# Folding a MoE output projection into the expert weights on chip, during the convolution

## What is computed

```
def _L3_ffn_ref(X, We, be, Wr, br, Wo, bo):
    ...
    router_weights = jax.nn.softmax(router_logits, axis=-1)
    top_k_weights, top_k_indices = jax.lax.top_k(router_weights, TOP_K)
    expert_outputs = jnp.einsum('bsd,ehd->bseh', X, We) + be
    ...
    combined = jnp.sum(top_k_weights[..., None] * gathered, axis=2)
    out = jnp.einsum('bsd,hd->bsh', combined, Wo) + bo
    return out
...
    t = t + _L3_ffn_ref(_ln_t(t), L3_ffn_We, L3_ffn_be, L3_ffn_Wr, L3_ffn_br, L3_ffn_Wo, L3_ffn_bo)
```

## Time and profile before

| | us |
|---|---|
| time, median of 3 runs | 751.39 (750.92 to 751.60) |
| the profiled execution: its own time | 752.36 |
| the profiled execution: span of its instructions | 750.6 |
| PE busy in the span | 637.6 (85%) |
| DVE busy | 471.3 (63%) |
| ACT busy | 320.1 (43%) |
| POOL busy | 143.5 (19%) |

### The profile page before, as it was taken

How to read it: one execution, slowest core, us unless ns; L and a number is a source line. 1 busy time by engine, 2 the same in 40 slices (tenths; PEclk the granted TensorE clock), 3 DMA queues, 4 the chain that set the end, 5 groups by cost and what they waited for, 6 DMA issues and landing times.

```text
span 750.6 us, 11202 instructions
## 1 busy us (share of the span) xinstructions
PE 637.6 (85%) x4168; PEld 396.0 (53%) x4230; DVE 471.3 (63%) x1259; ACT 320.1 (43%) x545; POOL 143.5 (19%) x126
## 2 busy tenths in 40 slices
PE   6543666349699999999999989999999999999987
PEld 3411225236366666666666655565655656564543
DVE  4777555685776776676677675737567473746433
ACT  3254554015355556555555553433434244343110
POOL 2230001572533133212203212020201100000000
PEclk9766777678799999999999999999999999999999
DMA  9300001986774995796597588246090730000000
GB/s 354 134 0 0 0 0 17 124 106 91 68 104 74 85 115 82 65 126 88 65 107 101 83 71 106 22 86 56 22 120 1 110 32 15 1 14 1 15 5 24
DMA packets 83230, 50.53 MB, mean 67 GB/s; under 512 B 4036, under 2 KB 82628, under 8 KB 82884
## 3 DMA queue, kind: packets, MB, share of 16 engines
q1 hardware_dynamic: 83176, 49.81, 46.8%
HBM read 35.11 MB, written 14.68 MB: 66 GB/s over the span
## 4 chain that ended last, share of the span: by engine, by line
PE 62%; DVE 10%; ACT 4%; issue 3%; DMA 2%; SPq 1%; POOL 0%; DVEq 0%; ACTq 0%
PE ps L1145 13%; PE ps L1031 10%; PE ps L1022 7%; PE ps L1091 4%; PE ps L1102 4%; PE ps L1087 3%; PE ps L1070 3%; PE ps L1062 3%; PE ps L1116 3%; DVE acc L1376 2%; PE ps L1014 2%; DVE nparts L1311 2%; PE ps L1156 2%; PE ps L1109 2%; PE ps L1065 2%
## 5 line engine op out<-in xcount | busy, mean ns | idle before, releaser
L1302 DVE TENSOR_REDUCE nmax<-ps 128x2 f32<-128x512 f32 (+1 forms) x192 | 130.7, 688 | 103.5 <-PE ps L1070 62.4
L1198 ACT ACTIVATE PT<-ps 128x512 f32<-128x512 f32 x192 | 114.9, 600 | 120.9 <-PE ps L1091 118.9
L1145 PE MATMUL ps<-wm,xnT 128*128 128x512 f32 x256 | 124.6, 616 | 0.6
L958 POOL TENSOR_TENSOR rstd<-ve,fix 128x2 f32<-128x2 f32 x32 | 22.2, 695 | 356.2 <-DVE ve L1264 356.2
L1192 ACT ACTIVATE QS<-ps 8x1024 bf16<-8x1024 f32 x64 | 65.1, 1017 | 40.2 <-PE ps L1075 39.4
L1376 DVE SCALAR_TENSOR_TENSOR acc<-ps,gate,acc 128x256 f32<-128x256 f32 x128 | 61.6, 481 | 29.6 <-PE ps L1145 27.3
L1091 PE MATMUL ps<-QS,KS 110*128 110x256 bf16 (+3 forms) x512 | 74.7, 248 | 0.0
L994 POOL TENSOR_TENSOR parts<-rest,fix 128x512 bf16<-128x512 f32 x30 | 38.1, 1269 | 159.9 <-DVE rest L1282 105.7
L1145 PEld LDWEIGHTS ps<-wm,xnT 128*128 128x128 f32 x256 | 45.9, 193 | 41.3 <-issue 39.0
L1022 PE MATMUL ps<-xnT,wt 128*128 128x256 f32 x256 | 65.5, 403 | 1.4 <-ACT xnT L1171 1.4
L1087 PE MATMUL ps<-fixb 128*128 128x256 bf16 (+1 forms) x192 | 60.6, 316 | 0.5 <-ACT QS L1192 0.3
(11 more groups left out here) (195 smaller groups left out, 967.9 us busy)
## 6 DMA issues: line engine op xcount, KB each, us to landing
parts_dram<-parts SPq DMA_DIRECT2D x32, 384.0 KB, 3.2
QS<-parts_dram SPq DMA_DIRECT2D x96, 128.0 KB
KS<-parts_dram SPq DMA_DIRECT2D x96, 128.0 KB, 9.8
wt<-wt_dram SPq DMA_DIRECT2D x1, 2562.0 KB, 13.1
wm<-wm_dram SPq DMA_DIRECT2D x1, 2449.0 KB, 18.4
xc<-x_dram SPq DMA_DIRECT2D x8, 256.0 KB, 5.0
out_dram<-res SPq DMA_DIRECT2D x8, 256.0 KB, 2.1
w<-w_dram SPq DMA_DIRECT2D x1, 845.0 KB, 7.4
```

The costliest lines, as they stand in the source:

```text
L1145: mm = pe.matmul(d, normT(stage, batch)[:, c, t * P:(t + 1) * P], M("We", c * EXPERTS * CH + e * 2 * CH, 2 * CH), start=(c == 0), stop=(c ...
L1198: act.activation(PT[:, n % PT_RING, :], bank(piece), ACT.Exp).then_inc(drain(piece), 1)
L1302: dve.tensor_reduce(group[:, 0, :] if part == 0 else group[:, 1, 2 * part - 2:2 * part], bank(piece).rearrange("p (j n) -> p j n", n=w_), ...
```

## The change

Wo is multiplied into the eight experts' weights and into the biases once, during the convolution block. Per expert PE transposes its four 128x128 blocks (turn_expert), ACT copies them to SBUF, PE multiplies them with Wo in four products of 128x256 (fold_expert), and ACT copies the result back over the expert's place in wm. PSUM banks for this are picked from those that the convolution leaves free at the time (TURN_BANK, FOLD_BANK); SBUF comes from tensors whose contents are no longer needed (xp, ph, pool_w). The load of wm is issued ahead of that of wt.

In the transformer block the piece FO is gone with its products, its ACT copy and its bank. CT now writes the result itself: ACT drains it with the two bias steps. The residual, which FO's identity products added, is added when acc is opened: GB is drained by DVE (acc = PSUM + xt) and no longer by ACT. The expert products themselves are as before, over changed contents of wm.

```diff
-        ("E", 3, 5, 39), ("E", 3, 6, 40), ("E", 3, 7, 41), ("CT", 3, 0, 43), ("FO", 3, 0, 45)),
+        ("E", 3, 5, 39), ("E", 3, 6, 40), ("E", 3, 7, 41), ("CT", 3, 0, 43)),
...
+            turned_we = (xp[:, 0, :], xp[:, 1, :], ph[:, :])
+            turned_be = pool_w[:, 0, 0:NC2 * EXPERTS]
+            TURN_BANK = (2, 3, 4, 6, 7, 0, 6, 3)
+            FOLD_BANK = (5, 2, 0, 1, 2, 4, 5, 6)
...
+                sp.dma_start(wm[:], wm_in).then_inc(wm_loaded, 16)
                 sp.dma_start(wt[:], wt_in).then_inc(wt_loaded, 16)
-                sp.dma_start(wm[:], wm_in).then_inc(wm_loaded, 16)
...
+                def turn_expert(e):
+                    for hh in range(NC2):
+                        for c in range(NC2):
+                            mm = pe.transpose(ps[:, TURN_BANK[e], hh * CH + c * P:hh * CH + (c + 1) * P],
+                                              expert(e)[:, c, hh * P:(hh + 1) * P], F("ident"))
+                    mm.then_inc(fold_turned, 1)
+                def fold_expert(e):
+                    pe.wait_ge(fold_turned_out, e + 1)
+                    for c in range(NC2):
+                        for hh in range(NC2):
+                            mm = pe.matmul(ps[:, FOLD_BANK[e], c * CH:(c + 1) * CH],
+                                           turned_we[e % 3][:, hh * CH + c * P:hh * CH + (c + 1) * P],
+                                           M("Wo", hh * CH, CH), start=(hh == 0), stop=(hh == 1))
+                    mm.then_inc(fold_done, 1)
...
+                pe.wait_ge(wm_loaded, 16)
+                for e in range(3):
+                    turn_expert(e)
+                pe.wait_ge(g_out, 1)
+                for e in range(2):
+                    fold_expert(e)
                 pe.wait_ge(weights_ready, 1)
...
+                fold_expert(2)
                 pe.wait_ge(tern_summed, 1)
...
+                for e in range(3, 6):
+                    pe.wait_ge(z_out, e - 2)
+                    turn_expert(e)
+                pe.wait_ge(z_out, 4)
+                fold_expert(3)
+                pe.wait_ge(z_out, 5)
+                fold_expert(4)
                 pe.wait_ge(z_out, 8)
+                turn_expert(6)
+                turn_expert(7)
+                fold_expert(5)
+                fold_expert(6)
                 all_max(0, 1)
+                fold_expert(7)
...
-                if kind == "GB":
-                    full(act, piece)
-                    full(act, ("CT", stage, batch - 1, 0))
-                    copy_out(flat(acc))
...
+                if kind == "GB":
+                    full(dve, piece)
+                    full(dve, ("CT", stage, batch - 1, 0))
+                    dve.tensor_tensor(flat(acc), bank(piece), flat(xt[:, par]), ALU.add).then_inc(drain(piece), 1)
...
                 if kind == "CT":
-                    full(act, piece)
-                    full(act, ("FO", stage, batch - 1, 0))
-                    copy_out(flat(accT))
-                if kind == "FO":
                     full(act, piece)
                     wait(act, "out_stored", before(piece, 2))
```

More of the change, by code:

```diff
@@ L472, in _ @@
                     for q in range(4):
+                        if o == 0 and q == 2:
+                            pe.wait_ge(folded, 3)
                         if o == 0 and q == 3:
@@ L496, in _ @@
                     mm.then_inc(conv_done, 1)
+                pe.wait_ge(fold_turned_out, 9)
+                for c in range(NC2):
+                    mm = pe.matmul(ps[0:EXPERTS, BE_FOLD_BANK, 0:CH], turned_be[:, c * EXPERTS:(c + 1) * EXPERTS],
+                                   M("Wo", c * CH, CH), start=(c == 0), stop=(c == 1))
+                mm.then_inc(fold_done, 1)
                 all_max(1, 2)
+                pe.wait_ge(folded, 9)
                 for k, (src, wgt) in enumerate(((hp1, dwq), (hp2, w2q))):
@@ L527, in _, with expert_turned, expert_folded @@
             def _(act):
+                def expert_turned(e):
+                    act.wait_ge(fold_turned, e + 1)
+                    act.activation(turned_we[e % 3], ps[:, TURN_BANK[e], :], ACT.Copy).then_inc(fold_turned_out, 1)
+                def expert_folded(e):
+                    act.wait_ge(fold_done, e + 1)
+                    act.activation(expert(e), ps[:, FOLD_BANK[e], :].rearrange("p (c n) -> p c n", c=NC2),
+                                   ACT.Copy).then_inc(folded, 1)
                 act.wait_ge(w0_loaded, 16)
@@ L854, in build @@
             acc = lb("acc", [P, 2, CH])
-            accT = lb("accT", [P, NC2, PIX])
             res = lb("res", [P, 2, NC2, PIX])
@@ L946, in sync_piece @@
                             .then_inc(sems[f"stack_loaded{n}"], 16)
-                if kind == "FO":
+                if kind == "CT":
                     wait(sp, "out_stored", before(piece))
@@ L1150, in tensor_piece @@
                     mm = turn4(acc)
-                if kind == "FO":
-                    drained(pe, ("CT", stage, batch, 0))
-                    for o in range(NC2):
-                        for c in range(NC2):
-                            pe.matmul(d[:, o * PIX:(o + 1) * PIX], M("Wo", c * CH + o * P, P), accT[:, c, :],
-                                      start=(c == 0), stop=False)
-                        for t in range(2):
-                            mm = pe.matmul(d[:, o * PIX + t * P:o * PIX + (t + 1) * P], xt[:, par, t, o * P:(o + 1) * P],
-                                           F("ident"), start=False, stop=(t == 1))
                 if kind in JOBS:
@@ L1325, in vector_piece @@
                     if kind == "PR" and stage == 2:
-                        full(dve, ("FO", 3, batch - 2, 0))
+                        drained(dve, ("GB", 3, batch - 2, 0))
                     old = flat(X[:, 2 * batch:2 * batch + 2, :])
```

47 lines of the change are left out of this document (41 added, 6 removed).

## The result

| | before | after |
|---|---|---|
| median of the runs timed side by side, us | 751.22 (750.92 to 751.60) | 729.20 (728.43 to 729.73) |
| the profiled execution: own time / span | 752.36 / 750.6 | 728.74 / 727.0 |
| from the span's start to batch 0's GB products | 448.10 | 448.19 |
| from there to the end | 302.5 | 278.8 |

A forecast was written before the change was run, and what follows sets the result against it. TensorE was taken to bound the second half, while the convolution waits on DVE and ACT. Terms -21.8 + 0 + 0 + 0.1 - 1.7 + 0.9 = -22.5 us gave 729.0 us, range 725.0 to 735.0.

The forecast's parts named there:

- Part 1: Transformer block: dropping FO saves 2.61 us in each of seven batches and 3.57 us at the end, -21.8 us.
- Rival B: Second half: PE's gain is half given back because DVE or the ring of six PSUM banks ends the waits; 739.8 us, chance 0.07.
- 42.0 us in the second half: Sign of being right: batch periods of 42.0 us in the second half, with PE still above 95% busy.
- Part 2: Transformer block: moving GB's drain from ACT to DVE costs 0 us, bounds -0.8 to +5.6 over 8 batches.
- Part 3: Convolution, before L451: folding experts 0 and 1 fits PE's idle 6.53 us, 0 us, bounds 0 and +2.3.
- Part 4: Convolution, PE's 1.62 us before L468: folding expert 2 at the full clock costs +0.1 us, bounds 0 and +1.8.
- Part 5: Convolution, z products: with the idle gap filled, four records no longer run at half clock, -1.7 us, bounds -1.7 and 0.
- Part 6: Convolution, around L481: folding experts 3 to 7, starting at the low clock, costs +0.9 us, bounds 0 and +6.5.
- A: Convolution: the clock does not follow, the first fold runs half at 1.2 GHz, z gains nothing; 733.7 us, chance 0.13.
- C: Convolution: the folding is not hidden at all, 35.5 us at half clock; 765 us, chance 0.02.
- D: Convolution: the clock stays up through folding experts 3 to 6, and first tap products start at full speed; 726.0 us, chance 0.12.
- E: Transformer block: FO was hidden anyway, so only the last batch's 3.6 us would go; 747.8 us, chance 0.02.

The follow-up runs named there:

- e4_slot: The changed kernel with one PSUM bank of the ring of six skipped where FO stood, nothing computed differently: 732.37 us, 0.9743 of before.
- experiment 4: Changed kernel with needless TensorE products before the last gate transposes (726.03 us), then with expert 2 early and expert 6 late too (725.14), then four more products (724.82).
- e3_gb_dve: The kernel before with only GB's drain moved from ACT to DVE, which adds the residual: 751.79 us, 1.0003 of before.
- e7_filler: The changed kernel with three needless 128x512 products on PE ahead of the last batch's gate transposes: 726.03 us, 0.9665 of before.
- e1_no_fold: Convolution block of before (no folding, Wo left out) with the transformer block of after: 727.59 us, 0.968 of before.
- e1_again: The kernel of e1_no_fold, without any folding, run once more beside the last experiments: 727.27 us, 0.9678 of before.
- after_again: The changed kernel itself, nothing altered, run once more beside later experiments: 729.82 us, 0.9705 of before.
- e2_fold_only: Convolution block of after, with all of the folding, and the transformer block of before, FO included: 751.47 us, 1.0005 of before.
- e10_all_warm: e9_all plus four more needless 128x512 products behind the transposes of experts 3 to 5: 724.82 us, 0.9642 of before.
- e9_all: Changed kernel with expert 2 folded before sc's transposes, expert 6 behind the first all_max, three needless products before the last gate transposes: 725.14 us, 0.9649 of before.

## Why the prediction was right, part by part

The profiled execution lost 752.36 - 728.74 = 23.6 us, where the sum said 22.5. By stretches it is 23.7 in the transformer block (21.8 predicted) and +0.1 in the convolution (-0.7 predicted). The total came out well partly because errors of the terms stood against each other.

- **Part 1, FO (-21.8): right.** The periods of e4_slot show 2.61 to 2.63 us a batch, and the end lost 3.58 where 3.57 was predicted. What the step left out is the ring: it took the loss of a job as free of side effects, and the loss gave 0.38 or 0.39 us more in each of four periods, 1.5 us. Rival B had looked at the ring, and thought of it as a loss. The working of "42.0 us in the second half" missed for the same reason: 41.63. A further part of the block's 23.7 is the clock. Six FOs lie between GB 1 and GB 7, 15.7 us; with the ring's 1.5 that makes 17.2, and the periods lost 18.8. The remaining 1.6 is nearly all in the seventh, which lost 4.16 us: before had a stretch at the low clock there (0.57 on the mean of 696 to 700). From GB 7 to the end FO of batch 6 and the tail should have given 2.61 + 3.57 = 6.2, and gave 28.2 - 23.3 = 4.9: after had the clock at 0.50 for the 6.7 us of the table in experiment 4, before only for half as long (723.6 to 726.9, at 0.50). These two nearly cancel.
- **Part 2, GB (0): right.** e3_gb_dve shows it alone: the periods of before, and 1.0003.
- **Part 3, experts 0 and 1 (0): right.** PE was done with them at 27.3 and still waited 1.62 us for DVE ahead of L490. The weights were there when PE asked, at 22.19.
- **Part 4, expert 2 (+0.1): mis-sized.** I priced it at the full clock, because the clock of before was 1.00 in that stretch. In after it was 0.50 from 30.5 on, and the fold took 3.10 us: z started 19.46 us behind the scores and not 17.88, so +1.6, close to the bound of +1.8. In e4_slot and e7_filler it was +1.4 and +1.7, in the four other traces with that order +0.2 to +0.4.
- **Part 5, z's clock (-1.7): right in size, wrong in what it is measured against.** z took 7.11 us and not 8.81. But the block of before does that too in half of its traces (e1_no_fold, e1_again), so the one trace of before that I read overstated the gain for the median. A stall of this kind, which hangs on where the clock happens to rise, is not a fixed price.
- **Part 6, experts 3 to 7 (+0.9): right in kind, and not one price.** The folding held the all_max up by 0.65 us in after and by 2.0 in after_again, inside the bounds of 0 and +6.5 on either side of the forecast. I had put L481's counterpart within 1 us of 58.4 and it came at 59.70, because z had started late.

Parts 3 to 6 together: -0.7 predicted. Against the same block when its z also runs at the full clock they cost 41.0 - 38.9 = +2.1 us to the first all_max; in the times it is +1.6 to +2.0 by the kernels without folding and +0.4 by e2_fold_only. So the convolution was worse than forecast by 1.1 to 2.8 us, the transformer block was better by 23.7 - 21.8 = 1.9 us, and the errors nearly cancel in the median: that it came within 0.2 us of the forecast is in part luck. One of my own signs of being wrong, a longer convolution although z got faster, did show, if faintly: +0.1 us to batch 0's GB, with z at 7.11.

**The rivals.** A (733.7): its clock behaviour came half true (expert 2 at half speed), at another place and smaller. By the Trainium skill, page "TensorE: Matmul & The Clock Gate", Part 4 (PE-mode transpose), transposes do not count as work for the clock. After has a stretch of 5.4 us in which PE does nothing but the transposes to tokens, from 113.36 on, and behind it the clock is at 1.00, as in the earlier trace rows:

```profile
113.50:118.90 5.40, 5.40 (x26) 5.40 (x27) 4.38 (x8) 5.22 (x9) 0.00 (x0) 0.50 0.00 0
119.50:121.00 1.50, 0.43 (x4) 0.19 (x2) 0.71 (x2) 0.60 (x1) 0.00 (x0) 1.00 0.00 0
```

So the trace disagrees with the page again, and the measurement decides. B (739.8) fell: PE's waits in 450 to 660 did not grow. C (765) fell: folding alone made 1.0005. D (726.0) was not what the changed kernel does, and its mechanism pays little: e10_all_warm kept the clock up through the folding of experts 3 and 4, and DVE then ended the wait (experiment 4). That e9_all and e10_all_warm are below 726.0 comes from other places, the tail above all. E (747.8) fell, since five periods lost FO's 2.61 us each and not only the last batch.

**What stays open.** From the first all_max to batch 0's GB the traces range from 387.2 to 388.9 us, with and without the folding, and the clock rises and falls at other places in each; I didn't settle which of it follows from the change. The price of the folding is open between 0 and about 2 us: 1.6 to 2.0 rests on two pairs of kernels whose intervals overlap a little, e2_fold_only says 0.4 with an interval up to 1.4, and the 2.1 us of the traces compares fast executions without the folding with others.

## What to carry to other kernels

Work moved from a stage where TensorE is the bound into a stage that waits is gained nearly in full (here 21.8 us, reckoned from one timeline, against at most about 2 us of new cost), and what is left of the cost sits where the moved pieces stand directly in front of a result that others wait for: put them ahead of a wait that ends on another engine, or behind the critical product (e9_all). When a job leaves a ring of buffers, all its neighbours change partners; skip a slot to find out what that alone is worth. And look at the granted clock in front of the last chain of a program: here a wait of 2.19 us cost 3 us more behind it, and three products that nobody reads kept the engine at full speed.

## What the runs showed of the hardware that I had not expected

- The clock's rises and falls are not at fixed places of a program: with the same instructions on PE, z's 16 records took 8.81 us in two traces and 7.11 us in two others, and y's took 3.78 us in after and 3.51 us in after_again. The medians of before itself went from 750.9 to 752.0 us between the three groups of experiments, each of which ran on another chip.
- A tiny DVE step can last as long as a big one of POOL beside it. Twice per execution, in before as in after, a step of 128x8 elements takes 6.9 us, five more times 1.0 us, and the other 57 times 0.17 us. The seven long ones each start just behind the start of a POOL step and end with it:

```profile
157.18 0.17 DVE L1390 TENSOR_TENSOR nparts<-nmax,nparts 128x8 bf16<-128x8 f32 x1
161.28 6.89 DVE L1390 TENSOR_TENSOR nparts<-nmax,nparts 128x8 bf16<-128x8 f32 x1
...
161.13 7.01 POOL L1074 TENSOR_TENSOR KS<-fixb 8x4096 bf16<-8x4096 bf16 x1
...
181.87 1.17 POOL L1095 TENSOR_TENSOR parts<-rest,parts 128x512 bf16<-128x512 f32 x1
182.05 1.01 DVE L1390 TENSOR_TENSOR nparts<-nmax,nparts 128x8 bf16<-128x8 f32 x1
```

In after all seven end 0.02 to 0.03 us behind POOL's, and none of the short ones overlaps a POOL step. In before one short step starts 0.02 us ahead of a POOL step, at 156.20, and isn't lengthened. That the POOL step is the cause is still an inference from starts and ends; no run took it away. The Trainium skill, page "SBUF — State Buffer", section "SBUF: two separate sides", says that the two engines share a pair of ports as an exclusive lock, which one holds for its whole instruction while the other is blocked, also for a DVE operation with two SBUF inputs when the POOL operation reads SBUF. The trace agrees: the DVE step reads nmax and nparts, the POOL step reads fixb, and DVE's ends 0.03 us after POOL's (168.17 against 168.14).
